# Quantised feed-forward rows packed on POOL and transposed by a DMA, in an attention and feed-forward kernel

## What is computed

```python
def act_quant(x):
    scale = 127.0 / jnp.clip(jnp.max(jnp.abs(x), axis=-1, keepdims=True), 1e-05)
    return jnp.clip(jnp.round(x * scale), -128, 127) / scale

def _L0_ffn_ref(x, w1, conv_w, conv_b, w2):
    h = bit_linear(x, w1)                       # 256 -> 1024, both sides quantised
    h = depthwise_conv1d(h.transpose(0, 2, 1), conv_w, conv_b)   # 3 taps along the tokens
    h = h.transpose(0, 2, 1)
    h = jax.nn.silu(h)
    return bit_linear(h, w2)                    # 1024 -> 256, rows of h quantised
x = x + _L0_ffn_ref(_layernorm(x, axis=-1), w1, conv_w, conv_b, w2)
```

## Time and profile before

| | |
|---|---|
| median of 3 runs | 440.6 us |
| profiled execution, its own time | 440.44 us |
| its span, first to last instruction | 438.6 us |
| mean granted TensorE clock | 0.995 of full speed |
| busy over the span: PE, DVE, ACT, POOL | 93%, 87%, 71%, 20% |
| chain of work that ended last, by engine | PE 52%, DVE 28%, ACT 13% |
| DMA, mean over the span | 51 GB/s |

### The profile page before, as it was taken

The page is one execution under the profiler, slowest core; times in us unless marked ns, Lnnn a source line. Parts: engine busy times, 40 slices in busy tenths (PEclk is TensorE's granted clock), DMA queues, the critical chain, the costliest instruction groups (busy, mean ns, idle before and its releaser), DMA issues.

```text
span 438.6 us, 13812 instructions
## 1 busy us (share of the span) xinstructions
PE 406.9 (93%) x5914; PEld 275.8 (63%) x5914; DVE 380.7 (87%) x602; ACT 310.1 (71%) x359; POOL 86.0 (20%) x115
## 2 busy tenths in 40 slices
PE   1999997799999999999999999999999988899985
PEld 1666675466667666666666666676666744576663
DVE  4789987989987889879879889889879899999994
ACT  2456777576888756766766767667766689999984
POOL 2175554940000120020120020111001010221200
PEclk9999999999999999999999999999999998999999
DMA  7702000612111111211211111111101000001002
GB/s 225 214 1 73 1 1 1 226 42 73 39 50 39 63 39 40 73 37 39 67 33 51 61 39 49 64 39 37 51 25 52 1 1 0 2 26 48 25 25 78
DMA packets 27587, 22.51 MB, mean 51 GB/s; under 512 B 7232, under 2 KB 27268, under 8 KB 27524
## 3 DMA queue, kind: packets, MB, share of 16 engines
q1 hardware_dynamic: 26112, 21.59, 15.3%
q10 hardware_dynamic: 1412, 0.01, 0.2%
HBM read 6.91 MB, written 2.10 MB: 21 GB/s over the span
## 4 chain that ended last, share of the span: by engine, by line
PE 52%; DVE 28%; ACT 13%; issue 3%; DMA 3%; ACTq 0%; DVEq 0%; POOL 0%; SPq 0%
DVE arena L721 16%; PE sc L1684 13%; PE heads L1701 6%; PE heads L1702 4%; PE heads L1703 4%; PE heads L1510 4%; ACT arena L1296 4%; PE sc L1521 3%; ACT qq L1372 3%; PE by L1589 2%; PE bx L1521 2%; ACT qq L1380 2%; PE by L1521 2%; PE sc L1788 2%; DMA lng<-in_L_xattn_ln_x_b 2%
## 5 line engine op out<-in xcount | busy, mean ns | idle before, releaser
L1296 ACT ACTIVATE arena<-sc,kb 128x1024 f32<-128x1024 f32 x160 | 169.7, 1112 | 73.4 <-PE sc L1684 73.3
L721 DVE SCALAR_TENSOR_TENSOR arena<-arena 128x1024 bf16<-128x1024 f32 x160 | 193.7, 1242 | 28.3 <-ACT arena L1296 27.3
L1701 PEld LDWEIGHTS heads<-v,arena 128*128 128x128 bf16 x1280 | 117.0, 97 | 40.8 <-issue 28.3
L1701 PE MATMUL heads<-v,arena 128*128 128x65 f16 x1280 | 130.6, 194 | 4.9 <-DVE arena L721 4.6
L1702 PE MATMUL heads<-v,arena 128*128 128x64 f16 x1280 | 129.7, 195 | 0.0
L1703 PE MATMUL heads<-v,arena 128*128 128x65 f16 x1280 | 129.1, 192 | 0.0
L1684 PE MATMUL sc<-qs,kst 64*128 64x512 f16 x960 | 118.0, 378 | 2.3 <-DVE kk L663 1.5
L1702 PEld LDWEIGHTS heads<-v,arena 128*128 128x128 bf16 x1280 | 118.8, 97 | 0.1
L1703 PEld LDWEIGHTS heads<-v,arena 128*128 128x128 bf16 x1280 | 118.8, 99 | 0.0
L1684 PEld LDWEIGHTS sc<-qs,kst 64*128 64x128 f16 x960 | 40.1, 94 | 48.2 <-issue 5.0
L518 POOL TENSOR_SCALAR frs<-fmv 128x2 f32<-128x2 f32 x8 | 7.9, 990 | 150.9 <-DVE fmv L795 150.9
(11 more groups left out here) (213 smaller groups left out, 586.7 us busy)
## 6 DMA issues: line engine op xcount, KB each, us to landing
kst<-kk SPq DMA_DIRECT2D x80, 128.0 KB, 2.0
xs<-in_x SPq DMA_DIRECT2D x8, 256.0 KB, 5.3
qs<-qq SPq DMA_DIRECT2D x16, 128.0 KB, 2.0
out<-cbuf SPq DMA_DIRECT2D x7, 256.0 KB, 2.1
xs<-in_ctx SPq DMA_DIRECT2D x6, 256.0 KB, 6.3
xs<-in_L_ffn_w SPq DMA_DIRECT2D x1, 1024.0 KB, 5.8
cbuf<-in_L_ffn_w SPq DMA_DIRECT2D x1, 1024.0 KB, 9.2
arena<-in_L_xattn_W_kv SPq DMA_DIRECT2D x2, 256.0 KB, 4.8
```

The lines of the kernel that those rows point to most:

```text
L721: e.scalar_tensor_tensor(out=rest[:, j, :, :], in0=prob[:, j, :, :], scalar=SHRINK, in1=probh[:, j, :, :], op0=ALU.mult, op1=ALU.subtract) ...
L1296: a_.activation(prob[:, j, :, :], sc[(j + 1) % 2][:, :, :], ACT.Exp, bias=kb[:, bass.ds(i * QUAD + j, 1)]).then_inc(exp_done[j], 1)
L1701: t_.matmul(o, hi, row[:, 0:OW], start=first and sub == 0, stop=False, skip_group_check=True)
```

## The change

In blocks 0 to 2 (tiles m = 0 to 11) `hidden_first` and `whole` are gone. In their place POOL reads every second fp16 number of `uf`, subtracts 1536, and packs them into a new SBUF buffer `uh` (two buffers, 128x1024 fp16, 256 KB each). SP then issues a DMA transpose from `uh` to `uq`, both in SBUF. Block 3 keeps `hidden_first` and `whole`.

```diff
+        MOVED = (NF - 1) * FT
+        by_dve = [MOVED + 2]
         def taken(m):
+            if m < MOVED:
+                return moved[m % 2], m // 2 * 16 + 16
...
+            def turn_hidden(m):
+                sp.wait_ge(s["packed"], m + 1)
+                wait(sp, "o_ps", m - 1)
+                sp.dma_start_transpose(uq[m % 2].rearrange("p (j c) -> p j c", j=J), uh[m % 2]).then_inc(moved[m % 2], 16)
+
+            for m in range(2 * BT - 1):
+                turn_hidden(m)
             for n in range(NB - 1):
                 sp.wait_ge(s["res_ready"], n * BT + BT)
                 sp.dma_start(outt[:, n * BT:(n + 1) * BT, :], ores[n % 2]).then_inc(stored[n % 2], 16)
+                for m in range((n + 2) * BT - 1, (n + 3) * BT - 1):
+                    if m < MOVED:
+                        turn_hidden(m)
...
+            def pack(m):
+                pool.wait_ge(s["uf_ready"], m + 1)
+                wait(pool, moved[m % 2], m // 2 * 16)
+                g.tensor_scalar(uh[m % 2], uf[m % 2].bitcast(F16)[:, 0:2 * HID:2], -HALF_AT, None, ALU.add).then_inc(s["packed"], 1)
             for n in range(NF):
                 for t in range(FT):
                     scale_back(n, t)
+                    if n < NF - 1:
+                        pack(n * FT + t)
```

`quantize` waits, before it writes a `uf` buffer again, for `packed` in place of `uqt_ps`. `tokens_first` waits for `uf_ready` of the tile that had its PSUM tile before, in place of `uq` being written:

```diff
-                if turned_before(n, t) >= 0:
+                if turned_before(n, t) >= MOVED:
                     pe.wait_ge(*taken(turned_before(n, t)))
+                elif turned_before(n, t) >= 0:
+                    pe.wait_ge(s["uf_ready"], turned_before(n, t) + 1)
```

More of the change, by code:

```diff
@@ L218, in xattn_ffn @@
         uq = [qf[:, 2 * HID + n * HID // 2:2 * HID + (n + 1) * HID // 2].bitcast(F16) for n in range(2)]
+        uh = [qf[:, 3 * HID + n * HID // 2:3 * HID + (n + 1) * HID // 2].bitcast(F16) for n in range(2)]
         ores = [cbuf[:, (2 + n) * BT * D:(3 + n) * BT * D].rearrange("p (t d) -> p t d", t=BT) for n in range(2)]
@@ L232, in xattn_ffn @@
             rstd2_ready dq_ready xd_ps xd_ready h_ps edge_ps center_ready left_ready taps_done edge_step edge_done
-            u_ready row_step ut_ps scale_step scale_pool scale_back uscale_ready uscale_late uf_ready uqt_ps uq_ready uq_late0 uq_late1 o_ps res_ready pad_done passed""".split()
+            u_ready row_step ut_ps scale_step scale_pool scale_back uscale_ready uscale_late uf_ready uqt_ps uq_ready uq_late0 packed o_ps res_ready pad_done passed""".split()
         s = {n: sem(n) for n in names}
@@ L247, in xattn_ffn @@
         stored = [sem(f"stored{i}") for i in range(2)]
+        moved = [sem(f"moved{i}") for i in range(2)]
         block = es.enter_context(nc.Block())
@@ L282, in turned @@
             return (n * FT + t) % 2 if n < NF - 1 else (2, 0, 1, 2)[t]
-        by_dve = [(NF - 2) * FT + 3, (NF - 1) * FT + 2]
+        MOVED = (NF - 1) * FT
+        by_dve = [MOVED + 2]
         def taken(m):
+            if m < MOVED:
+                return moved[m % 2], m // 2 * 16 + 16
             if m in by_dve:
-                return s[f"uq_late{by_dve.index(m)}"], 1
-            return s["uq_ready"], m + 1 - sum(k < m for k in by_dve)
+                return s["uq_late0"], 1
+            return s["uq_ready"], m - MOVED + 1 - sum(k < m for k in by_dve)
         def turned_before(n, t):
@@ L1084, in feed_forward @@
                 largest(3, 0)
-                whole(2, 3)
                 result(2, 2)
@@ L1370, in quantize @@
                     act.wait_ge(s["uscale_late"], m + 1 - BY_POOL)
-                wait(act, "uqt_ps", m - 1)
+                if m < MOVED + 2:
+                    wait(act, "packed", m - 1)
+                else:
+                    act.wait_ge(s["uqt_ps"], m - MOVED - 1)
                 a_.activation(uf[t % 2], ut[turned(n, t)], ACT.Identity, scale=fu[:, 2, t:t + 1], bias=shifts[:, 0:1]).then_inc(s["uf_ready"], 1)
@@ L1431, in feed_forward @@
                     silu(n, 0)
-                    whole(n - 1, 0)
                     center_ahead(n, 5)
@@ L1437, in feed_forward @@
                     center_ahead(n, 7)
-                    whole(n - 1, 1)
                     quantize(n - 1, 2)
@@ L1441, in feed_forward @@
                     center_ahead(n, 8)
-                    if n < NF - 1:
-                        whole(n - 1, 2)
                     silu(n, 3)
@@ L1906, in feed_forward @@
                         second_product(n - 2, 3)
-                    hidden_first(n - 1, 0)
                     hidden_ahead(n, 5)
@@ L1911, in feed_forward @@
                     hidden_ahead(n, 7)
-                    hidden_first(n - 1, 1)
                     second_product(n - 1, 0)
@@ L1916, in feed_forward @@
                     hidden_ahead(n, 9)
-                    hidden_first(n - 1, 2)
                     second_product(n - 1, 1)
@@ L1923, in feed_forward @@
                 second_product(2, 2)
-                hidden_first(2, 3)
                 tokens_first(3, 1)
```

9 lines of the change are left out of this document (2 added, 7 removed).

## The result

The changed kernel takes 456.28 us (median of 4 runs, 455.95 to 456.58), the kernel before 440.50 on the same chip: a ratio of 1.035 with the interval from 1.0331 to 1.037, 15.7 us slower. The forecast was 446.7, with a range from 440.8 to 457.0. So the sign was right and the range holds the time, but the loss is two and a half times the 6.1 us that were worked out, and the time lies outside the forecast's own range, 443.5 to 451. That the whole range holds it is luck: its upper end is there for a queue of the transposes, and no such queue formed. The profiled execution has a span of 454.1 us where the one before had 438.6.

A forecast was written before the change was run, and what follows sets the result against it. DVE was taken as the bound, with PE and ACT nearly as full. A loss of 3.4 us in blocks 0 and 1 plus 2.7 in the last block, 6.1, on the median of 440.6 gave 446.7 us, range 440.8 to 457.

The forecast's parts named there:

- the forecast's own range: Main case, a transpose of 3.3 to 5.5 us and the wait at the port: 443.5 to 451 us, chance 0.45.
- a queue of the transposes: Rival: transposes follow one after the other and set the pace, 390.3 + 12d, for d = 5.6 us some 457; chance 0.15.
- the packing's size: POOL packing 1024 fp16 numbers per row in blocks 0 to 2: 1.2 us taken, bounds 1.0 and 6.4.
- the rival for a longer packing: Packing takes 1.8 us in place of 1.2: 3 us more at most, inside the range; no chance of its own.
- the sentence on the next tile's scale: POOL's scale of the next tile stands behind the packing, moving by half a microsecond, hidden by 0.8 us before ACT came.
- The threshold of the forecast: Packing and transpose together under 3.3 us: DVE never waits; from there each microsecond costs one in each of three blocks.
- The transpose: SP's transposing DMA of 256 KB, from issue to landing: 4.4 us, the middle of 2.1 and 6.8.
- The port: DVE's edge_taps(n, 2), with two SBUF inputs, waits for POOL's packing: 0.94 us per block, 2.8 in all.
- its 1.3 us of idle time: DVE's idle time in three stretches, 0.60, 0.65 and 0.07 us: the most that ACT's and PE's savings can bring.
- the longer distance between blocks: Sign: from one block's first largest to the next's grows from 18.0 to some 19 us or more.
- the port's sign: Sign: some edge_taps(n, 2) stand behind an idle time of DVE that ends with POOL's packing.
- The last block's loss: Block 2's port wait, 0.94 us, plus PE 1.8 us late at second_product(2, 3), delaying the whole last block: 2.7 us.

The follow-up runs named there:

- scale on DVE: Changed kernel with the row scales of all tiles made on DVE instead of POOL, packing unchanged: 448.98 us, ratio 1.0195.
- no packing: Changed kernel with ACT writing the rounded row directly as fp16 and the product taking off the 1536, so POOL packs nothing: 440.10 us, ratio 0.9992.
- 128 numbers: Changed kernel with only 128 of the 1024 columns packed, the transpose still moving all: 440.45 us, ratio 1.0004.
- 512 numbers: Changed kernel with only 512 of the 1024 columns packed, the rest left out: 444.04 us, ratio 1.008.
- copy as packing: Changed kernel packing by a plain POOL copy, the 1536 taken off by one more matmul per tile: 444.08 us, ratio 1.0087.
- the two kernels with a copy: Changed kernel packing by a POOL copy, 444.08 us; and the one where ACT writes fp16 directly, plus one idle POOL copy per tile, 444.39 us.
- the kernel with the filler: Changed kernel with 24, 24, 24 and 16 overwritten matmuls in PE's waits before second_product of tiles 2, 6, 10 and 11: 456.65 us, ratio 1.0357.

## Why the prediction was right and wrong

**The step that failed is the packing's size.** It was taken at 1.2 us, near the lower bound of 1.0, which came from copies and a conversion, and the upper bound of 6.4, from the one POOL tensor_scalar of some length in the trace, was set aside as disturbed by DVE. The packing measured 2.79 us, and 1.04 where it was a copy: the lower bound was right for a copy and said nothing of a tensor_scalar. The upper row was disturbed, as the prediction said: by the slope measured here 256 numbers take 0.87 us and not 1.6 (an estimate, 0.23 + 256 x 2.50 ns). But the reason given for taking a value near the lower bound, that DVE doesn't slow POOL in the FFN, only removes the disturbance. It doesn't say that an undisturbed tensor_scalar costs what a copy costs, and that step had no row. Even the rival for a longer packing went only to 1.8.

**With it fell the sentence on the next tile's scale**, "hidden" at half a microsecond. POOL's operations for one tile were priced one by one and the loop through POOL, ACT and POOL was not closed: 0.25 + 0.58 of scale, 1.21 of `quantize`, 2.79 of packing and the gaps make 5.08 us a tile, against DVE's 17.4 / 4 = 4.35. With the packing at 1.2 the loop would be 3.5 us and the sentence would hold. This term is worth about 7 us: 15.7 less the 8.9 of the kernel with the scale on DVE, which has some work of its own added.

**The threshold of the forecast held, roughly.** It said that packing and transpose together have 3.3 us, and that from there each microsecond costs one in each of three blocks. With the durations that the runs gave:

```
kernel                 packing + transpose   3 x (sum - 3.3)   measured, us
no packing             0    + 3.0             0                 -0.1
128 numbers            0.55 + 3.0             0.8                0.4
copy                   1.04 + 3.0             2.2                3.8
512 numbers            1.51 + 3.0             3.6                3.8
scale on DVE           2.77 + 3.1             7.7                8.9
```

That also is the cost in the kernel of 512 numbers that the loop couldn't explain. With 2.79 + 3.1 the rule gives 7.8 us for the changed kernel. The other 7.9 are the queue on POOL and PE's lower clock. The measured column holds what the lower clock costs in the slower kernels, and the row of the copy the port's waits, so that the fit is this close is in part chance.

**The lower clock of PE** stands in no term of the sum. It comes with the waits that the change makes, and on the chain of the changed kernel it is 2.8 of the 15.7 us. It also stands in the other slower kernels: from 421 to 426 us the granted clock is 1.00 before and without packing, 0.86 with 512 numbers packed and 0.50 with the copy as packing.

**The transpose** was taken at 4.4 us between 2.1 and 6.8 and measured 3.1, inside the bounds and nearer to the plain store. The estimate of 2.6 us by the Trainium skill, DMA: Bandwidth & Descriptors, on the anatomy of one DMA, was closer than the middle of the bounds; the Trainium skill gives that fit for DMAs issued from GpSimd, and these are issued from SP. The statement of the Trainium skill, Advanced Engine Details and Errata, section X-Bar Transpose (TRN2), that such a transfer is as fast as a regular one holds only roughly here: 3.1 us against 2.4 for the same bytes. The two errors, 1.6 too little in the packing and 1.3 too much in the transpose, nearly cancel in their sum, 5.6 us forecast and 5.9 measured, which is luck; the kernel without the queue on POOL, with the scale on DVE, lost 8.9 us for the 6.1 forecast.

**The port** was taken at 2.8 us and cost nothing: in the changed kernel all sixteen `edge_taps` took 0.148 to 0.161 us, and none of them began inside a packing. The queue on POOL had moved the packing away from them: that of (1, 2) starts 6.1 us behind its `largest` and not 3.5, and `edge_taps(2, 2)` 4.6 and not 3.8. That a wait exists was right, at 0.61 to 0.87 us each in the two kernels with a copy, and with PE's clock it explains why the copy as packing still lost 3.8 us. From one block's first `largest` to the next's and to the end:

```
kernel                 block 0   block 1   the rest, us   port's waits in each
before                 17.61     17.97     31.69          none
no packing             17.36     17.58     31.64          none
copy                   18.01     18.26     34.50          0.61, 0.62, 0.87 + 0.61
```

Blocks 0 and 1 with the copy are longer than those without packing by the port's wait and nothing else, 0.65 and 0.68. The 1.04 + 3.0 of packing and transpose cost nothing beside it, since a DVE that has waited also wants the result later; the rule's 2.2 us and the waits don't add up. The rest is longer by 2.86, the waits of 1.48 and some 1.4 in which PE's product and `tokens_first` take 1.71 and 1.72 us on the chain.

**What was right:** DVE is the bound, and its 1.3 us of idle time is all that the removed work could bring. The kernel without packing got 0.1 us, which can't be told from nothing. PE's and ACT's 16 us of removed work bought nothing. Of the signs named, the longer distance between blocks, `result(n-1, 2)` behind the product and the product behind the DMA all came, at 3 to 4 us each; the port's sign, the packing's 1.0 to 1.8 us and the transposes' 4.4 did not. The last block's loss, 5.3 us for the predicted 2.7, has the same causes, as the chain from 417 on goes through the same loop, and 1.4 us of it are the lower clock.

**What stays open:** why PE's clock fell after one wait and not after another as long; its cost is read from the chains, and no run changed the clock and nothing else. And why single transposes took up to 4.6 us in the kernel with the filler and up to 5.1 in the others, where the median is 3.0 to 3.1.

## What to carry to other kernels

Don't price an operation by a row of another operation with the same bytes; where the rows nearest to it are far apart, say what the time would be at either end before choosing. Work put on an engine with idle time is priced by what stands behind it in that engine's order: close the loop from one tile to the next through all engines and compare it with the bound's time per tile. Work taken from engines beside the bound brought nothing here, however much it was. And where an experiment adds work to fill a wait, look at the chain for the filler itself before reading the time.

## What the runs showed of the hardware that was not expected

- POOL with 128 partitions: a tensor_scalar takes 0.23 us + 2.50 ns per number, from rows of 128, 512 and 1024 numbers. At 1024 it is alike for strided fp16, dense fp16 and dense fp32. A copy of 1024 strided fp16 takes 1.04 us.
- The port's wait isn't as long as POOL's operation. Inside copies of 1.04 us an `edge_taps` ended with the copy. Inside tensor_scalars it ended sooner. In the kernel of 512 numbers and in the one with the scale on DVE (POOL's row and DVE's, each):

```profile
403.15 1.51 POOL L583 TENSOR_SCALAR qq<-qq 128x512 f16<-128x512 f16 x1 [1.17 <-ACT qq L1398]
...
403.33 0.45 DVE L969 TENSOR_TENSOR v<-v,edges 128x4 f32<-128x4 f32 x1
```

```profile
383.68 2.77 POOL L583 TENSOR_SCALAR qq<-qq 128x1024 f16<-128x1024 f16 x1 [0.60 <-ACT qq L1398]
...
384.78 0.16 DVE L969 TENSOR_TENSOR kk<-kk,edges 128x4 f32<-128x4 f32 x1
```

  The first ends 0.63 us into POOL's 1.51, and the second, begun at 1.10 of 2.77, waits for nothing. Both would fit a port that is held for about as long as a copy of as many numbers takes (0.60 and 1.04 us), which no run tests by itself.
- A transpose of 128x1024 fp16 from SBUF to SBUF occupies SP's queue for 1.23 us and a plain copy of it for 0.51; back to back a transpose holds it for 1.32.
- PE's matmuls at either level of the clock: the eight matmuls of a product take 1.05 us at the full clock and 1.89 on the chain where the granted clock of the stretch is 0.50 to 0.57. Waits of 3.18 and 3.19 us stood ahead of one at each level in the same kernel.
